# Two-layer cross attention: the loads of the next context and of the next pair's rows, issued by ScalarE instead of SyncE

## What is computed

```python
q = hidden @ Wq + bq;  k = context @ Wk + bk;  v = context @ Wv + bv
scores = einsum('bkgld,bksd->bkgls', q, k) * scale + mask
attn = softmax(scores)
out = einsum('bkgls,bksd->bkgld', attn, v) @ Wo + bo
x = layer_norm(out + hidden) * gamma + beta
```

## Time and profile before

| | |
|---|---|
| median of three runs | 1748.52 us |
| the profiled execution | 1741.95 us |
| its span | 1739.7 us |
| PE busy | 1688.4 us (97%) |
| DVE busy | 1276.0 us (73%) |
| ACT busy | 1041.3 us (60%) |
| POOL busy | 569.2 us (33%) |
| SP's queue (q1) | 204.79 MB, 44.6% of the 16 DMA engines |
| ACT's queue (q10) | 30.41 MB, 7.1% of the 16 DMA engines |

### The profile page before, as it was taken

One profiled execution on the slowest core, in us unless ns is written; L12 is line 12 of the kernel. 1 busy time (PEld: TensorE's weight loads), 2 busy tenths in 40 slices (PEclk: granted clock), 3 DMA queues, 4 the chain that ended last, 5 costly groups with the idle time before them and its releaser, 6 DMA issues. The chain is left out here.

```text
span 1739.7 us, 35820 instructions
## 1 busy us (share of the span) xinstructions
PE 1688.4 (97%) x10881; PEld 1004.5 (58%) x10881; DVE 1276.0 (73%) x1717; ACT 1041.3 (60%) x2370; POOL 569.2 (33%) x1167
## 2 busy tenths in 40 slices
PE   4899999999999999999999999999999999999996
PEld 2565566565566565565665565665565655665652
DVE  6577777787777787776787776777776777776775
ACT  1465666566666566665656665666665666665663
POOL 1233332333332333332333332333333333323322
PEclk8999999999999999999999999999999999999999
DMA  7656545455545455546465444455454455454441
GB/s 240 179 144 160 151 120 143 135 132 146 149 117 143 136 135 146 148 119 154 125 151 145 121 129 131 114 139 146 108 134 130 118 134 150 106 133 130 121 117 46
DMA packets 288393, 235.87 MB, mean 136 GB/s; under 512 B 140858, under 2 KB 262964, under 8 KB 288084
## 3 DMA queue, kind: packets, MB, share of 16 engines
q1 hardware_dynamic: 266420, 204.79, 44.6%
q10 hardware_dynamic: 21920, 30.41, 7.1%
HBM read 101.39 MB, written 22.02 MB: 71 GB/s over the span
## 5 line engine op out<-in xcount | busy, mean ns | idle before, releaser
L823 DVE TENSOR_REDUCE mx<-ms 128x2 f32<-128x750 f32 x896 | 809.5, 925 | 405.4 <-PE ms L962 399.2
L682 ACT ACTIVATE probs<-sc 125x448 f32<-125x448 f32 x1520 | 743.0, 542 | 285.4 <-PE sc L933 279.2
L962 PE MATMUL ms<-ks,qs 96*128 96x375 bf16 (+1 forms) x2560 | 438.4, 325 | 18.8 <-DMA qs<-qp 10.2
L933 PE MATMUL sc<-qs,ks 99*125 99x448 bf16 x1520 | 426.9, 357 | 3.5 <-DMA qs<-mT 2.1
L981 PE MATMUL pv<-probs,vs 125*32 125x448 f32 x3072 | 315.2, 543 | 0.0
L933 PEld LDWEIGHTS sc<-qs,ks 99*125 99x125 bf16 x1520 | 192.0, 136 | 200.4 <-ACT probs L682 122.0
L962 PEld LDWEIGHTS ms<-ks,qs 96*128 96x128 bf16 (+1 forms) x2560 | 174.3, 98 | 197.5 <-issue 73.5
L1024 PE MATMUL job<-wo,on 128*112 128x512 f32 x512 | 263.1, 596 | 4.8 <-POOL on L578 4.8
L1041 PE MATMUL job<-xT,wq 128*128 128x224 f32 x1024 | 217.5, 356 | 0.9 <-ACT qf L724 0.9
L837 DVE RECIPROCAL orec<-osum 128x112 f32<-128x112 f32 x256 | 213.2, 835 | 0.9 <-DMA osum<-oraw 0.9
L1041 PEld LDWEIGHTS job<-xT,wq 128*128 128x128 f32 x1024 | 190.2, 190 | 20.2 <-ACT qf L724 8.3
(11 more groups left out here) (57 smaller groups left out, 1027.5 us busy)
## 6 DMA issues: line engine op xcount, KB each, us to landing
ctxT<-in_ctxT SPq DMA_DIRECT2D x64, 750.0 KB, 4.8
qs<-qp SPq DMA_DIRECT2D x750, 56.0 KB, 2.5
ks<-kp SPq DMA_DIRECT2D x768, 46.9 KB, 2.9
osum<-oraw ACTq DMA_DIRECT2D x128, 112.0 KB, 2.9
oc<-oraw ACTq DMA_DIRECT2D x128, 112.0 KB, 3.9
mask<-in_mask SPq DMA_DIRECT2D x64, 164.1 KB, 5.6
xT<-in_xT SPq DMA_DIRECT2D x32, 224.0 KB, 4.6
xin<-in_x SPq DMA_DIRECT2D x32, 224.0 KB, 3.1
```

The costliest lines, as they stand in the source:

```text
L682: nc.scalar.activation(probs[0:KCS, k, j, :], bank[0:KCS, 0:GL], ACT.Exp)\
L823: nc.vector.tensor_reduce(mx[o][:, cols], ms[n % 2][:, :, 0:S2], AX_X, ALU.max).then_inc(max_done[o], 1)
L933: last = nc.tensor.matmul(bank[0:KCS, 0:GL], ks[p][0:KM, g, rows], qs[p][0:KM, g, :], start=True, stop=not masked)
L962: last = nc.tensor.matmul(to, qs[o][0:KT, group, cols], ks[o][0:KT, group, :], start=True, stop=not masked)
```

## The change

The two helpers `load_ctx` and `load_xT` get a copy on ScalarE, with the same waits, and the calls move from the end of SyncE's slot to the end of ScalarE's slot, behind the exponentials of piece 11 (and, in p = 0 slots, behind `osum` and `oc`, which are issued in the same piece). The opening slots (i = −1) still load on SyncE. All semaphores, buffers and sizes stay.

```diff
@@ SyncE, slot
-                more = not isinstance(ahead, int) or 0 <= ahead + 1 < UNITS
...
-                if more:
-                    load_ctx(o, ahead + 1, lay[3] if not isinstance(ahead, int) else 0 if ahead + 1 < PER else 1)
-                if p == 1 and (not isinstance(proj, int) or 0 < proj + 1 < UNITS):
-                    after = lay[3] if not isinstance(proj, int) else 0 if proj + 1 < PER else 1
-                    for u in range(PAR):
-                        load_xT(u, proj + 1, after)
                 if isinstance(i, int) and (p, i) == (0, 0):
                     load_rows(1, w_in[1])
@@ ScalarE
+            def count(value):
+                return value if isinstance(value, int) else act.snap(value)
+
+            def batch(p, n, layer):
+                return count(2 * n + p - B * layer)
+
+            def load_ctx(p, n, layer):
+                b, before = batch(p, n, layer), count(n)
+                need(act, v_ps[p], before)
+                need(act, k_ps[p], before)
+                act.dma_start(ctxT[p][:, :, :].rearrange("p a b -> p (a b)"), ctxT_d[b]).then_inc(ctx_in[p], 16)
+
+            def load_xT(p, n, layer):
+                b, before = batch(p, n, layer), count(2 * n)
+                turned = count(16 * SQUARES * (n - PER) + 16 * SQUARES) if layer == 1 else 0
+                need(act, q_ps, before)
+                need(act, yT_out[p], turned)
+                if layer == 0:
+                    src = xT_d[b].rearrange("p (a b) -> p a b", a=DC)
+                else:
+                    src = yT_d[b].rearrange("(a q) p l -> (q p) a l", a=DC)
+                act.dma_start(xT[:, :, p, :], src).then_inc(xT_in[p], 16)
@@ ScalarE, slot
+                def loads():
+
+                    if not isinstance(ahead, int) or 0 <= ahead + 1 < UNITS:
+                        load_ctx(o, ahead + 1, lay[3] if not isinstance(ahead, int) else 0 if ahead + 1 < PER else 1)
+                    if p == 1 and (not isinstance(proj, int) or 0 < proj + 1 < UNITS):
+                        after = lay[3] if not isinstance(proj, int) else 0 if proj + 1 < PER else 1
+                        for u in range(PAR):
+                            load_xT(u, proj + 1, after)
...
                 if opens(p, i):
                     send_queries()
+                else:
+                    loads()
```

## The result

The changed kernel takes 1799.9 us (median of four runs, 1794.06 to 1806.05) against 1748.33 us before, a ratio of 1.0313 with a 95% interval of 1.0286 to 1.034. The profiled execution is the one of 1798.03 us with a span of 1795.9 us, 56.2 us more than before.

A forecast was written before the change was run, and what follows sets the result against it. PE was taken as the limit, busy 97% of the span. Four context loads without slack, 2.8 us, plus 0.5 us for row loads made 3.3 us on 1748.52, so 1751.8 us; range 1745 to 1766.

The forecast's parts named there:

- What bounds the kernel: PE limits every part of the slot; the change can remove a few us at most but add waits at 62 turns.
- SyncE relieved: SyncE's mask and stacks move up 0.7 us at one turn, about 2.0 at the other; worth 0 to 0.3, taken 0.
- ScalarE's issue time: Piece 0's exponentials slip 0.2 to 1.0 us at one turn, 1.1 to 1.9 at the other, covered; cost 0.
- The shift: At the p = 0 to p = 1 turn the context's issue moves back 0.6 to 1.0 us, taken as 0.7.
- The 2.8 us at four loads: Four of 31 context loads at the p = 0 to p = 1 turn had no slack; each waits 0.7 us more.
- The flight: Context at the p = 0 to p = 1 turn still lands about 5 us after issue; 1.0 us of slack left.
- The sum: Four context loads without slack, 2.8 us, plus row loads, 0.5 us: 3.3 us added to 1748.52 us.
- Rival A: Context late at every p = 0 to p = 1 turn, sharing evenly with mask and stacks: 16 us, 1768 us; chance 0.17.
- Its mild end: Mild forms of the late-context rival, 0.1 us per turn, were counted as falling within no measurable change.
- The evidence I weighed against A: `oc`, issued 0.2 us before a context, landed after 5.7 us, 3.3 without one: small transfers wait for the large one.
- The row loads: Three 224 KB bias and scale loads now leave SyncE before the first context without slack; 0 to 2.5 us, taken 0.5.

The follow-up runs named there:

- e2: Changed kernel, but SyncE keeps the p = 0 slots' context load; ScalarE issues only the p = 1 slots' context and xT loads; 1747.09 us, 1.0001.
- e5: Changed kernel, but ScalarE issues the p = 0 slots' context in piece 8, some 6 us earlier than at the slot's end; 1745.25 us, 1.0002.
- e3: Kernel before, all loads on SyncE, plus a wait for the next slot's first scores before the p = 0 slots' context issue; 1747.75 us, 0.9995.
- e11: Changed kernel with the mask of the p = 1 slots moved behind the twelve stacks, no hold; 1755.22 us, 1.0063.
- e13: Changed kernel, every issue in place, but the mask of parity-0 items carries 16 of 112 rows, 24 KB instead of 164 KB; 1759.51 us, 1.0079.
- e14: Changed kernel with the p = 1 slots' mask between the six key and six query stacks, some 3 us after the context; 1754.58 us, 1.0057.
- e9: Changed kernel, but in p = 0 slots ScalarE issues the context in piece 11 ahead of osum and oc, about 1.3 us earlier; 1751.09 us, 1.0033.
- e12: Changed kernel with osum and oc of the p = 0 slots issued in piece 10 instead of 11; 1773.62 us, 1.0157.
- e8: Changed kernel, but in p = 1 slots SyncE holds the twelve stacks until the context has landed; 1874.36 us, 1.0693.
- e6: Changed kernel, but the three loads of the second layer's bias and scale rows are issued a slot later; 1797.97 us, 1.0311.
- e7: Changed kernel, but the twelve stacks at the start of p = 1 slots carry 4 source rows instead of 64; 1756.42 us, 1.0063.
- e10: Changed kernel; p = 1 slots' stacks held until piece 0's exponentials are done, and the mask moved behind the stacks; 1774.51 us, 1.0176.
- e4: Changed kernel; in p = 1 slots SyncE holds the twelve stacks, behind the mask, until piece 0's exponentials are done; 1796.73 us, 1.0261.
- e1: Changed kernel, but SyncE keeps the p = 1 slots' context and xT loads; ScalarE issues only the p = 0 slots' context; 1803.47 us, 1.0311.

## Why the prediction was wrong, point by point

**What bounds the kernel: right.** PE is the limit, a gain of more than a few us wasn't there, and every wait added at a turn was paid in full.

**SyncE relieved: worth 0, right.** e2 and e5 take three or four loads a pair off SyncE and don't get faster. What I priced as harmless, though, was the other side of it: that the mask and then the twelve stacks move up by 0.7 us. I asked only who waits for them, and not what they collide with. The mask and the first stack moved from behind the context to ahead of it, and that collision is the loss.

**ScalarE's issue time: cost 0, right.** The slip is 0.64 us at one turn, with no wait behind it. At the other turn e2 has a slip of 1.4 us (1.79 us from PE's scores of piece 0 to the exponentials, 0.39 before), at no cost.

**The shift: 0.7 us taken, 0.7 measured.** The context leaves 0.9 us later within the slot: `oc` took 0.86 us to issue, the end I hadn't taken, since with the context gone from SyncE the mask was issued beside it. But PE's place of use comes later too, and from issue to use the median shrinks by 6.58 − 5.84 = 0.74 us. e3 has that shift alone and costs nothing. In e11, e13 and e14, where PE isn't held up, the shift is 0.9 us (5.68 us from issue to use); with an undisturbed flight they cost 0.6 to 0.8%, 10 to 14 us. PE's waits for contexts are 17 to 20 us there against 8.9, and 3.6 to 5.0 us of that are the first load alone, which has the row loads ahead of it. What the later loads wait is 3.8 to 7.4 us against 0.8. The 2.8 us at four loads were too small there: five to seven later loads wait instead of two, among them loads with a long flight now and then (3.09 us of wait at 830.5 in e11).

**The flight: the step that failed.** The sum carried the flight of 4.9 us over to a place where the neighbours are different. It measured 7.0 there, 1.8 us more in the median, and with it all 31 loads wait instead of four. Rival A was this case, with a chance of 0.17. It had the place right (every p = 1 slot) and the extra flight nearly (1.5 us), but not the mechanism: it said even sharing with mask and stacks together, and e11 shows that full stacks ahead and beside add nothing to the 5.1 us of before. That its 1.5 us came so near was partly luck. Its price of 16 us beyond the forecast was too low for four reasons: 1.8 to 2.1 instead of 1.5 us of flight; a slack of 1.46 us in the median, where the turn it was read from has 1.7; 4.7 us at the first load; and about 8 us of lower clock, which no rival had. Its mild end didn't exist.

**The evidence I weighed against A.** `oc`, issued 0.2 us ahead of a context, landed late, and I read that as a large transfer that isn't cut into. The comparison was weaker than I made it: the `oc` that landed after 3.3 us wasn't without a context beside it, one was issued 1.2 us behind it. The pair of rows shows only that 0.2 us of lead is too little and 1.2 us enough. The runs bear the reading out where the context starts first: in e9 and e12 its flight is 5.46 and 4.92 with mask and stacks close behind. But it says nothing of a large transfer that starts behind another. I had written that no row shows the reverse case, and took the small price all the same. The rule of the Trainium skill (DMA: Bandwidth & Descriptors, section Queues, rings and completion order), that the engines go round the queues by whole packets, was used to support that. With the mask ahead alone it fits: 5.3 us in e8, with the data 0.6 us later than before. With mask and stacks both, the context isn't let through after one small transfer: 7.0 us. The measurement decides, and by it the rule isn't enough to price this case.

**The row loads: 0.5 us taken, with 2.5 as the upper end; mis-sized.** The flight of the load behind them went from 5.5 to 9.0 us, 3.5 us more, and PE waited 4.72 us for it instead of 0.31. That separate queues would keep the rows out of the context's way isn't borne out: it takes 7.8 to 9.2 us wherever the rows leave ahead of it, also in the kernels whose other loads are undisturbed. e6 takes off only 0.5 us, but puts the mask in the rows' place; how much is the rows' alone stays open.

## What to carry to other kernels

Moving a transfer to another issuing engine moves it in time and changes what stands ahead of it; its old flight holds only for its old neighbours. Give the transfer with the least slack a price for flight at both ends, and before changing its issuer list what its old queue will now send in front of it. The remedy is slack: six microseconds earlier the same move is free (e5), and putting one unhurried load behind the urgent ones took back four fifths of the loss (e11, 1.0063 against 1.0313). In e11 the first load's wait of 4.96 us, behind the row loads, is about half of what PE still waits more for contexts than before (19.7 against 8.9 us).

## What the runs showed of the hardware

The unexpected part is that two kinds of traffic, each of which leaves the flight near the 5.1 us of before, delay it by a third together. A 750 KB load behind a 164 KB one alone takes 5.3 us (e8), behind and beside twelve transfers of 47 to 56 KB 5.1 us (e11), and with both 7.0 us, with its 16 completions 2.3 us apart. Behind two loads of 224 KB, with a third beside it, the same load takes 7.8 to 9.2 us (the first load of e7, e8, e10, e11, e13 and e14).

PE's waits of 2.5 to 4.7 us in the changed kernel stood on or right before stretches of 3.4 to 6.8 us at half the granted clock, while its waits up to 2.0 us for contexts had none behind them. That is no sharp line: in e4 waits of 1.85 and 1.88 us (up to 635.8 and 745.1) have such a stretch right behind them, in e1 one of 2.97 us (up to 1128.3) has none.
